# Second attention: transposes of the weights right ahead of the next scores, both token products of a cycle behind them in one piece

## The chip, the cores and the metric

One core of one Trainium2 chip runs the whole program. The time is that of one launch in device microseconds, the median of three runs. Five engines work side by side, each through its own list of instructions in order, and meet by semaphores alone: TensorE (PE, with its weight loads PEld), VectorE (DVE), ScalarE (ACT), GpSimd (POOL) and SyncE (SP, which issues DMAs).

## The reference, cut to what matters

Two transformer blocks over x of shape (2, 1024, 256), 16 heads of 16. Each has two attentions and an MLP. The change touches the second attention of the first block, and the products that run beside it:

```python
def _topk_cross_attn(h, ctx, w_q, b_q, w_kv, b_kv, w_co, b_co):
    ...                                    # q from 1024 tokens, k and v from 154 context rows
    scores = jnp.einsum('bqhd,bkhd->bhqk', q, k) / jnp.sqrt(jnp.float32(D)).astype(h.dtype)
    top_s, top_i = jax.lax.top_k(scores, TOPK)          # 16 largest of 154
    attn = jax.nn.softmax(top_s, axis=-1)
    vg = jnp.take_along_axis(v_bh[:, :, None, :, :], top_i[..., None], axis=3)
    o = jnp.einsum('bhqk,bhqkd->bqhd', attn, vg).reshape(B, L, C)
    return o @ w_co + b_co
```

## The kernel before, in words

All matrices are float32. The work of the four attentions and of the stages between them (output projection, layer norm, projections, MLP; "token work" below) is written as small steps. `make_plan` gives every step a due time with `plan.at` or `plan.fill`; `Plan.finish` sorts all steps by due time, ties by the order in which they were added, gives each PE step a PSUM bank, and every engine then walks the one sorted list and carries out its own part of each step. So the due times are no delays: they set nothing but the order in each engine's queue.

The second attention (`topk_run`) takes 64 cycles, one for each group of four heads and tile of 128 queries. Call them k = 0 to 63, and let k.5 be a due time half a cycle after the cycle's start (`step`, 5.2 in plan units). Of cycle k:

- PE, `c_scores` (L1156), due 0.8 cycle ahead: eight matmuls into two of the four banks 1 to 4, one bank for each half of the heads (hf 0 and 1). It waits until both banks have been left by the cycle two earlier: for VectorE's first replacement (L1575) and for `c_exp_all` of that cycle's second half.
- DVE, `c_top` at k.0 and k.5: largest eight, replace, largest eight, replace (L1572 to L1582) for two heads each. It waits for `c_neg` two halves back.
- ACT, `c_neg` (L1343) at k.12 and k.62, and `c_exp_all` (L1353) at k.25 and k.75: the negated maximum, and exp of all scores.
- POOL, `c_pick` (L1658, L1660) at k.55 and (k+1).05: keeps the weights of the picked scores.
- PE, `c_tail` and `c_turn` (L1167, L1175): transposes of the weights, into bank 7 and bank 5. ACT, `c_copy` (L1363, L1364), takes them out.
- After every fourth cycle PE `c_pv` (L1188, L1190) multiplies with the values into bank 7, ACT `o_copy` (L1338) takes the result out, PE `o_turn` (L986) transposes it, DVE `o_norm` (L1481, L1491) normalizes. The next `c_tail`, which writes bank 7 too, waits for `o_copy`.

The token work is put into these cycles by the helper `under` of `make_plan`: one slot a cycle in cycles 1 to 17 (`per` = 1), two a cycle in 19 to 63 (`per` = 2; call them A and B). A slot of the MLP is one product of four matmuls, `ua`, `ub` (both L1049) or `down` (L1064). What follows the product on ACT or DVE is in the same slot, but `fill` sets it later: by a quarter of a cycle for the kinds in `SOON` (ACT's copies: `ua_copy` L1298, `silu` L1314, `qk_a`, `v_copy`, `on_copy`, `modulate` L1264), by 0.9 for those in `LATE` (DVE's: `hid` L1527, `x_sum`, `stats`, `out_sum`, `qk_d` L1459), by half a cycle for `x_hat` (L1306). Token products use banks 0 and 6 here, as `o_turn` does. Where both still hold something whose follow-up stands later in the list, `finish` pulls that follow-up forward.

In cycles 19 to 35 and 36 to 52 the token work is the output projection and MLP of the first batch element (halves n = 0 and 1), from slot 0 at 19A and 36A: `on_turn` 0, `y_mm` 2 and 3, `x_hat` 5, `hat_turn` 7, `ua` 9 to 16 (with `silu` after the fourth and the eighth), `ub` 17 to 24, `down` 25 to 32. Three products of the next stage (`qk`) lie in slots 5, 6 and 8 of the second. Cycles 53 to 58 hold the rest of that stage, 59 to 63 the first ten slots for the second batch element.

Of the kernel before, what the change touches and what calls it, by code (L numbers as in the profile page):

```python
# [467 lines left out]
def topk_run(plan, start, step):  # L468


    u = 0
    for b in range(B):
        for half in range(2):
            for g in range(GB):
                gi = 8 + b * GB + g
                for t in range(4 * half, 4 * half + 4):
                    t0 = start + u * step
                    sooner = (9.0, 4.0)[u] if u < 2 else 0.0
                    plan.at(t0 - 0.8 * step - sooner, ("c_score", gi, t, 0), ("c_score", gi, t, 1), ("c_scores", gi, t))
                    for hf in range(2):  # L480
                        t1 = t0 + 0.5 * hf * step
                        plan.at(t1 - (sooner if u == 0 else 0.0), ("c_top", gi, t, hf))
                        plan.at(t1 + 0.12 * step, ("c_neg", gi, t, hf))
                        plan.at(t1 + 0.25 * step, ("c_exp_all", gi, t, hf))
                        plan.at(t1 + 0.55 * step, ("c_pick", gi, t, hf))
                    plan.at(t0 + 1.9 * step, ("c_tail", gi, t), ("c_turn", gi, t))
                    plan.at(t0 + 2.0 * step, ("c_copy", gi, t))
                    if t % 4 == 3:
                        plan.at(t0 + 2.3 * step, ("c_pv", gi, half))
                        plan.at(t0 + 2.75 * step, ("o_copy", gi, half))  # L490
                        plan.at(t0 + 3.1 * step, ("o_turn", gi, half))
                        plan.at(t0 + 3.6 * step, ("o_norm", gi, half))
                    u += 1
    return start + u * step


def first_slots():

    s, b = 1, 0
    qk = lambda n, u: ("qk", s, b, n, u)  # L500
    out = lambda n, u: ("qk_d" if u % 2 else "qk_a", s, b, n, u)
    turns = lambda n: [("hat_turn", s, b, n, k) for k in range(CK)]
    modulate = lambda n: [("modulate", s, b, n, k) for k in range(CK)]
    x_hat = lambda n: [("x_hat", s, b, 2 * n), ("x_hat", s, b, 2 * n + 1)]
    first = [[("stats", s, b, 0), ("stats", s, b, 1), ("rstd", s, b, 0)] + x_hat(0) + [("stats", s, b, 2), ("stats", s, b, 3), ("rstd", s, b, 1)],
             [("prep",), ("mcol", 0), ("mcol_add", 0)], turns(0), modulate(0) + x_hat(1), [qk(0, 0)], turns(1), [out(0, 0)], [qk(0, 2)],
             modulate(1), [out(0, 2), qk(1, 0)], [out(1, 0), qk(1, 2)], [out(1, 2)]]
    left = []
    for n in range(2):
        left += [[qk(n, 1)], [out(n, 1), qk(n, 3)], [out(n, 3)]]  # L510
        for t in range(4 * n, 4 * n + 4):
            left += [[("v", s, b, t)], [("v_copy", s, b, t)]]
    return first, left


def make_plan():
    plan = Plan()
    first, left = first_slots()
# [25 lines left out]
    step = 5.2  # L544
    A2 = end + 3
    half = 16 * step
    end = topk_run(plan, A2, step)
    plan.at(A2 - 1.9, ("load_row", 1), ("load_gate", 2), ("load_out", 2), ("gate_out", 2))
    plan.at(A2 + 4, ("load_gate", 3))

    def under(first, last, slots, per, aside=0.3):
        return plan.fill(slots, [A2 + (first + (i + aside) / per) * step for i in range(int((last - first) * per))], (0.25 * step, 0.9 * step, 0.5 * step))

    under(1, 18, joined([gap_slots(2, 1, n) for n in range(2)]), 1)
    under(1, 7, late, 1, 0.8)
    plan.at(A2 + 8.5 * step, ("stash",), ("load_w", "m1"), ("load_w", "m2a"))
    for part in range(4):
        plan.at(A2 + (9.3 + part) * step, ("gate_m2", 0, part))
    plan.at(A2 + 18 * step, ("load_row", 2), ("load_gate", 4), ("load_out", 3), ("gate_out", 3), ("load_gate", 5), ("load_row", 3))
    plan.at(A2 + 19 * step, ("load_w", "wb1"))  # L560
    under(19, 36, in_turn([gap_slots(3, 0, 0, 1)]), 2)
    mlp = in_turn([gap_slots(3, 0, 1, 1)])
    (head0, tail0), (head1, tail1) = gap_slots(4, 0, 0), gap_slots(4, 0, 1)
# [19 lines left out]
    first, second = ([(head, tail[0:4:2]) for head, tail in four], [tail[1:4:2] + tail[4:] for _, tail in four])  # L583
    blocks = joined([([], (head + tail)[10:]), three[1]] + first)
    where = plan.fill(blocks, early)
    last = [i for i, slot in enumerate(blocks) if ("ub", 3, 1, 1, HT - 1) in slot][0]
# [1289 lines left out]
```

## Time and profile before

| | us |
|---|---|
| median of 3 runs | 1485.85 (1484.37 to 1489.32) |
| the profiled execution's own time | 1483.23 |
| its span | 1481.4 |
| PE busy | 1366.8 (92%) |
| DVE busy | 902.6 (61%) |
| ACT busy | 725.3 (49%) |
| POOL busy | 345.4 (23%) |
| clock granted to TensorE, mean | 0.966 |

The second attention lies about between 190 and 573 us of the span. A busy share is that of all instructions of the engine, and says nothing of what waits for what; "idle before, releaser" in a row says how long the engine stood still ahead of an instruction, and whose instruction let it go.

### The profile page before, as it was taken

How to read it: one execution, taken by the hardware profiler on the slowest of the kernel's cores; microseconds unless marked ns; L12 is line 12 of the kernel's file. 1: busy time of each engine (PE TensorE's matmuls, PEld its weight loads, DVE VectorE, ACT ScalarE, POOL GpSimd, SP SyncE). 2: the span in 40 equal slices, each digit the busy share in tenths (PEclk: the TensorE clock that was granted, in tenths of full speed). 3: DMA queues.
4: the chain of work that ended last, by engine and by line, in shares of the span. 5: the costliest groups of instructions: out<-in, count | busy, mean ns of one | idle time of the engine just before them, and what ended most of it. 6: DMA issues, size and time to landing. Idle time of an engine off the chain costs nothing.

```text
span 1481.4 us, 25463 instructions
## 1 busy us (share of the span) xinstructions
PE 1366.8 (92%) x9100; PEld 685.4 (46%) x9100; DVE 902.6 (61%) x2787; ACT 725.3 (49%) x1482; POOL 345.4 (23%) x397
## 2 busy tenths in 40 slices
PE   7999987888998997989899999999999999988998
PEld 5467654444644553442224333343433335544665
DVE  3556488877777785865465666676676345650320
ACT  2354555574474363125544565554556664443221
POOL 1021078875665675010000100001010011010220
PEclk9999987899999899999999999999999999999999
DMA  5101003000000000000002000000000000000000
GB/s 194 47 26 27 21 19 115 10 1 1 4 13 1 30 2 27 0 2 0 2 0 73 1 1 1 2 1 2 1 12 1 2 2 2 13 6 0 15 24 23
DMA packets 22094, 26.75 MB, mean 18 GB/s; under 512 B 4205, under 2 KB 19635, under 8 KB 21709
## 3 DMA queue, kind: packets, MB, share of 16 engines
q1 hardware_dynamic: 21059, 25.03, 5.2%
q8 instruction: 73, 1.20, 0.4%
q14 instruction: 53, 0.43, 0.1%
q10 hardware_dynamic: 909, 0.10, 0.0%
HBM read 21.58 MB, written 3.08 MB: 17 GB/s over the span
## 4 chain that ended last, share of the span: by engine, by line
PE 78%; DVE 11%; ACT 4%; issue 4%; POOL 2%; DMA 0%; ACTq 0%; SPq 0%; DVEq 0%; POOLq 0%
PE bank L1092 27%; PE bank L1049 11%; PE bank L1132 8%; PE bank L1064 7%; PE bank L1028 6%; PE bank L1007 3%; PE bank L986 2%; PE bank L1156 2%; PE bank L1034 2%; PE bank L1175 2%; DVE left L1575 1%; DVE x_hat L1520 1%; DVE stats L1507 1%; PE bank L1014 1%; DVE left L1582 1%
## 5 line engine op out<-in xcount | busy, mean ns | idle before, releaser
L1331 ACT ACTIVATE pr<-bank 128x512 f32<-128x512 f32 x656 | 353.4, 598 | 282.3 <-PE bank L1092 269.0
L1547 DVE TENSOR_REDUCE part_max<-bank 128x1 f32<-128x512 f32 x512 | 327.2, 685 | 182.4 <-PE bank L1092 181.9
L1092 PE MATMUL bank<-slot 32*128 32x512 f32 (+1 forms) x3072 | 386.1, 519 | 10.5 <-ACT pr L1331 6.1
L1092 PEld LDWEIGHTS bank<-slot 32*128 32x128 f32 x3072 | 160.7, 185 | 209.1 <-issue 157.3
L1599 POOL TENSOR_SCALAR var_eps<-mean_var 128x4 f32<-128x4 f32 x24 | 5.5, 227 | 889.9 <-DVE mean_var L1511 889.4
L1658 POOL TENSOR_SCALAR left<-left 128x308 f32<-128x308 f32 x128 | 125.2, 978 | 83.9 <-ACT exp_all L1353 41.7
L1132 PE MATMUL bank<-pr,v 128*17 128x512 f32 x1024 | 135.2, 600 | 0.2
L1049 PE MATMUL bank<-h_t,w_m 128*128 128x512 f32 x256 | 128.7, 629 | 4.7 <-DVE o_all L1491 3.2
L1660 POOL TENSOR_TENSOR probs<-left,exp_all 128x308 f32<-128x308 f32 x128 | 107.2, 838 | 10.7
L1572 DVE MAX8 top<-bank 128x8 f32<-128x154 f32 x256 | 69.7, 314 | 48.4 <-PE bank L1156 36.9
L1353 ACT ACTIVATE exp_all<-bank,neg 128x154 f32<-128x154 f32 x256 | 85.6, 386 | 6.7 <-DVE left L1575 2.1
L1551 DVE TENSOR_REDUCE neg_max<-bank 128x3 f32<-128x462 f32 (+1 forms) x96 | 50.7, 579 | 52.1 <-PE bank L1092 51.8
L1575 DVE MATCH_REPLACE8 left<-top,bank 128x154 f32<-128x154 f32 x256 | 77.0, 309 | 0.0
L1582 DVE MATCH_REPLACE8 left<-top,left 128x154 f32<-128x154 f32 x256 | 76.0, 305 | 0.4 <-issue 0.3
L1049 PEld LDWEIGHTS bank<-h_t,w_m 128*128 128x128 f32 x256 | 45.6, 197 | 65.4 <-issue 58.0
L1500 DVE TENSOR_TENSOR x_sb<-x_sb,bank 128x512 f32<-128x512 f32 x32 | 21.9, 685 | 84.1 <-PE bank L1007 84.1
L1064 PE MATMUL bank<-w_m,hidden 128*128 128x256 f32 x256 | 66.7, 407 | 6.6 <-DVE hidden L1527 6.5
L1364 ACT ACTIVATE probs_t<-bank 128x512 f32<-128x512 f32 x64 | 38.2, 597 | 63.9 <-PE bank L1175 63.6
L1338 ACT ACTIVATE o_st<-bank 128x512 f32<-128x512 f32 x64 | 38.3, 599 | 61.2 <-PE bank L1137 30.1
L1578 DVE MAX8 top<-left 128x8 f32<-128x154 f32 x256 | 68.2, 309 | 0.0
L1007 PE MATMUL bank<-w_out,o_norm_t 128*128 128x256 f32 x256 | 64.4, 396 | 1.4 <-DVE x_sb L1500 1.4
L1028 PE MATMUL bank<-h_t,wa 128*128 128x512 f32 x128 | 63.6, 626 | 2.0 <-ACT h_t L1264 1.9
(143 smaller groups left out, 1767.0 us busy)
## 6 DMA issues: line engine op xcount, KB each, us to landing
w_m<-in_L_xcond_w_m SPq DMA_DIRECT2D x1, 2048.0 KB, 7.6
w_m<-in_L_xcond_w_m SPq DMA_DIRECT2D x2, 1024.0 KB, 7.8
w<-in_L_xcond_w SPq DMA_DIRECT2D x2, 1024.0 KB, 6.6
w_ada<-in_L_xcond_w_ada SPq DMA_DIRECT2D x1, 1792.0 KB, 9.9
x_sb<-in_x SPq DMA_DIRECT2D x6, 256.0 KB, 6.3
res_row<-rows_dram SPq DMA_DIRECT2D x12, 128.0 KB, 3.3
out_x<-x_sb SPq DMA_DIRECT2D x6, 256.0 KB, 2.1
wa<-in_L_xcond_w_qkv SPq DMA_DIRECT2D x1, 768.0 KB, 6.6
```

The lines of the kernel that those rows point to most:

```text
L1007: last = nc.tensor.matmul(bank[:, tt * C:(tt + 1) * C], m.o_norm_t[:, slot, k, tt * P:(tt + 1) * P], m.w_out[:, j % 2, k, :], start=(k == ...
L1028: last = nc.tensor.matmul(bank[:, :], w[:, k, c0:c0 + P], m.h_t[:, slot, k, :], start=(k == 0), stop=(k == CK - 1))
L1049: last = nc.tensor.matmul(bank[:, :], w[:, k, c0:c0 + P], m.h_t[:, slot, k, :], start=(k == 0), stop=(k == CK - 1))
L1064: last = nc.tensor.matmul(bank[:, tt * C:(tt + 1) * C], m.hidden[:, j, t * P:(t + 1) * P], w, start=(j == 0), stop=(j == HT - 1))
L1092: last = nc.tensor.matmul(g.bank(*tile)[:, into], left, right, start=True, stop=True)
L1132: last = nc.tensor.matmul(out[h * HW:h * HW + VE, :], m.v[b][:, d % TB, heads[h], :], m.pr[:, slots[h], :], start=(d % TB == 0), stop=(d % ...
L1331: nc.scalar.activation(m.pr[:, u % NPR, :], g.bank("s", gi, i)[:, :], ACT.Exp).then_inc(g.free("s", gi, i), 1)
L1547: nc.vector.tensor_reduce(m.part_max[:, slot, h * TB + i // 8, i // 4 % 2:i // 4 % 2 + 1], bank[:, :], axis=AX.X, op=ALU.max).then_inc(don ...
L1575: nc.vector.match_replace(m.left1[:, v % 2, hh, :], m.top[:, v % 2, hh, 0:8], bank[:, hh * C:hh * C + S2], -FAR).then_inc(m.left1_done, 1)
L1582: nc.vector.match_replace(m.left2[:, v % 4, hh, :], m.top[:, v % 2, hh, 8:16], m.left1[:, v % 2, hh, :], -FAR).then_inc(m.left2_done, 1)
L1658: nc.gpsimd.tensor_scalar(left, left, -FAR, None, ALU.is_equal).then_inc(m.marked, 1)
L1660: nc.gpsimd.tensor_tensor(m.probs[:, u % 2, 2 * hf:2 * hf + 2, 0:S2], left, m.exp_all[:, v % 4, :, :], ALU.mult).then_inc(m.pick_done, 1)
```

## The change

In `topk_run` the transposes of cycle k's weights move from (k+1).9 to (k+2).12, and their copy from (k+2).0 to (k+2).16. The product with the values moves from .3 to .42 of its cycle, its copy from .75 to .8, and `o_turn` from .1 to .14. In `under` slots A and B, which were due at .15 and .65 of a cycle, are due at .30 and .32; with one slot a cycle the due time stays .3. The instructions are the same.

```diff
-                    plan.at(t0 + 1.9 * step, ("c_tail", gi, t), ("c_turn", gi, t))
-                    plan.at(t0 + 2.0 * step, ("c_copy", gi, t))
+                    plan.at(t0 + 2.12 * step, ("c_tail", gi, t), ("c_turn", gi, t))
+                    plan.at(t0 + 2.16 * step, ("c_copy", gi, t))
                     if t % 4 == 3:
-                        plan.at(t0 + 2.3 * step, ("c_pv", gi, half))
-                        plan.at(t0 + 2.75 * step, ("o_copy", gi, half))
-                        plan.at(t0 + 3.1 * step, ("o_turn", gi, half))
+                        plan.at(t0 + 2.42 * step, ("c_pv", gi, half))
+                        plan.at(t0 + 2.8 * step, ("o_copy", gi, half))
+                        plan.at(t0 + 3.14 * step, ("o_turn", gi, half))
                         plan.at(t0 + 3.6 * step, ("o_norm", gi, half))
...
     def under(first, last, slots, per, aside=0.3):
-        return plan.fill(slots, [A2 + (first + (i + aside) / per) * step for i in range(int((last - first) * per))], (0.25 * step, 0.9 * step, 0.5 * step))
+        return plan.fill(slots, [A2 + (first + i // per + aside + 0.02 * (i % per)) * step for i in range(int((last - first) * per))], (0.25 * step, 0.9 * step, 0.5 * step))
```

## Rows read from the trace of the kernel before

**Rows 1.** Stretches of the second attention: start:end, length, busy us of each engine, clock

```profile
215.00:285.00 70.00, 54.34 (x389) 30.39 (x389) 62.25 (x349) 42.76 (x121) 59.94 (x67) 0.88 0.20 66
285.00:410.00 125.00, 113.48 (x654) 65.98 (x652) 99.00 (x515) 69.35 (x179) 82.78 (x94) 0.89 0.01 2
```

**Rows 2.** Waits between 215 and 590 us: us in total, times, longest

```profile
POOL left L1658 <- ACT exp_all L1353: 41.7, 19, 7.6
DVE top L1572 <- PE bank L1156: 36.9, 22, 6.2
...
PE bank L1014 <- ACT x_hat L1306: 6.6, 3, 3.3
```

**Rows 3.** TensorE's timeline, one cycle of the MLP: start, us, instructions

```profile
443.65 0.42 PE L1167 MATMUL bank<-ident,probs 128*32 128x128 f32 x8
...
444.50 1.88 PE L1049 MATMUL bank<-h_t,w_m 128*128 128x512 f32 x4
446.31 0.79 PE L1156 MATMUL bank<-kc,slot 32*128 32x154 f32 x8
447.03 1.98 PE L1049 MATMUL bank<-h_t,w_m 128*128 128x512 f32 x4
448.95 0.42 PE L1167 MATMUL bank<-ident,probs 128*32 128x128 f32 x8
```

**Rows 4.** VectorE's timeline: two halves of `c_top` after one another

```profile
254.36 0.54 DVE L1572 MAX8 top<-bank 128x8 f32<-128x154 f32 x2
...
256.41 0.55 DVE L1572 MAX8 top<-bank 128x8 f32<-128x154 f32 x2
```

**Rows 5.** TensorE's timeline: transposes before scores, and two token products in one piece

```profile
244.58 0.66 PE L1175 MATMUL bank<-ident,probs 128*128 128x128 f32 x4
245.16 0.79 PE L1156 MATMUL bank<-kc,slot 32*128 32x154 f32 x8
...
590.32 3.70 PE L1049 MATMUL bank<-h_t,w_m 128*128 128x512 f32 x8
```

**Rows 6.** ScalarE's timeline in cycle 27 and 28, with two silus

```profile
335.72 0.69 ACT L1298 ACTIVATE hidden<-bank,columns 128x512 f32<-128x512 f32 x1 [0.33 <-PE bank L1049]
...
337.72 2.00 ACT L1314 ACTIVATE hidden<-hidden 128x1024 f32<-128x1024 f32 x2
339.63 0.19 ACT L1343 ACTIVATE neg<-top 128x2 f32<-128x2 f32 x1
339.83 1.28 ACT L1353 ACT_TABLE_LOAD   x1
341.13 0.67 ACT L1353 ACTIVATE exp_all<-bank,neg 128x154 f32<-128x154 f32 x2
```

**Rows 7.** TensorE's timeline in the same cycles; [idle before <-releaser]

```profile
335.61 0.79 PE L1156 MATMUL bank<-kc,slot 32*128 32x154 f32 x8
...
341.94 0.79 PE L1156 MATMUL bank<-kc,slot 32*128 32x154 f32 x8 [0.96 <-ACT exp_all L1353]
```

**Rows 8.** TensorE after a product with the values, no token product behind it

```profile
300.54 0.43 PE L1167 MATMUL bank<-ident,probs 128*32 128x128 f32 x8 [0.81 <-ACT o_st L1338]
```

**Rows 9.** TensorE at two token products that stand still

```profile
365.05 1.19 PE L1064 MATMUL bank<-w_m,hidden 128*128 128x256 f32 x2 [3.08 <-DVE hidden L1527]
...
511.47 3.78 PE L1034 MATMUL bank<-wa,h_t 128*128 128x256 f32 x8 [2.82 <-DVE slot L1459]
```

**Rows 10.** ScalarE and VectorE at waits in cycles 9 and 13

```profile
238.58 0.69 ACT L1276 ACTIVATE slot<-bank,columns 128x512 f32<-128x512 f32 x1 [3.32 <-PE bank L1028]
...
264.21 0.55 DVE L1572 MAX8 top<-bank 128x8 f32<-128x154 f32 x2 [3.45 <-ACT neg L1343]
```

**Rows 11.** TensorE in cycle 13

```profile
258.52 2.08 PE L1188 MATMUL bank<-tails_t,vt 128*128 128x512 f32 x2
...
261.87 1.09 PE L1014 MATMUL bank<-ident,x_hat 128*128 128x128 f32 x8
```

**Rows 12.** The stretch behind the stall at 365 us, as in Rows 1

```profile
365.00:371.00 6.00, 5.95 (x23) 4.35 (x24) 1.85 (x12) 0.52 (x2) 0.00 (x0) 0.54 0.01 3
```

## Prediction

> **What bounds the kernel now.** I read first the busy shares by stretch [rows 1]. In the cycles with one token slot VectorE is the busiest (62.25 of 70 us), in those with two TensorE is (113.48 of 125). The sums of waits [rows 2] show that the engines also wait in a ring: VectorE 36.9 us for scores, GpSimd 41.7 us for ScalarE's exp. Where a wait costs time must then be read from the queue orders and timelines.
>
> A cycle of the MLP without a stall [rows 3] is 448.95 − 443.65 = 5.30 us of TensorE, back to back: transposes 0.85 (0.35 + 0.50), token product 1.81, scores 0.72, token product 1.92. VectorE has 2 × 2.05 = 4.1 us of `c_top` in a cycle [rows 4] and needs more than that only with `ub`, where `hid` comes on top. So in `ua`, `qk` and `down` slots TensorE is the bound, and any new gap in it is lost.
>
> **The change part by part.** No instruction is added or removed, no DMA, and nothing moves on SP's queue. On POOL only `rstd` and `row` move, with their slots.
>
> *TensorE's work.* By the due times, two-slot cycles go from [transposes, A, scores, B] to [transposes, scores, A, B]. Transposes to scores take 0.35 + 0.58, two products in one piece 3.63 (3.70 less the 0.07 by which a row overlaps the next) [rows 5], scores 0.72: 5.28 against 5.30. The new piece is worth −0.02 a cycle, 0 to −1 over 45 cycles. In one-slot cycles TensorE's order stays, but for the values product (below).
>
> *The exp behind the token copies.* Scores of cycle k+2 need `c_exp_all` of (k, second half), due k.75. Before, slot A's ACT copy was due k.40 and B's k.90, behind that exp. Now they are due k.55 and k.57, both ahead of `c_neg` (k.62) and the exp. B's copy can only start when B is done, and TensorE has nothing but the transposes (0.93) left before it wants the scores. A copy starts 0.11 after its product (335.72 − 335.61) and takes 0.69, of which 0.09 overlaps what follows (339.72 − 339.63); `c_neg` takes 0.20, exp 0.67, and scores follow its end by 0.14 (341.94 − 341.80) [rows 6, 7]. That is 1.72 against 0.93: about 0.78 us of new stall in every cycle whose last token product has an ACT copy behind it. Such are 23, 24, 26, 40, 43, 63 (`ua`): 6 × 0.78 = 4.7. Nine more have a modulate, `qk_a`, `v_copy` or `on_copy` last (22, 36, 38, 39, 54, 55, 58, 59, 62), 0.8 to 1.5 each: 8.3. Sum 13. The ends are 0, if TensorE waits there for something later anyway, and 20.
>
> *The same with silu.* In cycles 25, 27, 42, 44 slot A has two silus with a table load, and the exp behind them needs a load back. From the copy's start to the scores let go, 341.94 − 335.72 = 6.22 [rows 6, 7]. Before, TensorE filled this with scores, B, transposes and the next A, and stood still 0.96 (1.07 at the most in the four). Now scores come before A and the next A is behind the next scores, so only B and the transposes (1.82 + 0.93) cover it: 0.11 + 6.22 − 2.75 = 3.6 us. Where B is a `ua`, its copy adds 0.6 (cycle 42: 4.2). In cycle 25 the values product covers some, but the next `c_tail` then waits for `o_copy` behind the exp: 3.5. Extra over before: 2 × 2.6 + 3.1 + 2.4 = 10.7. Ends 6 and 13.
>
> The trace has 1.28 us for the load, and the exp starts 0.02 after it [rows 6]. The Trainium skill (ScalarE: Activation LUTs, What ACT_TABLE_LOAD costs) has about 2.66 us for a switch, drain included. By that the four stalls would be some 2 × 1.38 longer each, 11 more; the row decides, and I take nothing for it.
>
> *Values product behind the tokens.* It was due .3, ahead of B; now .42, behind both, and the next `c_tail` in bank 7 wants its `o_copy` at once. Without a token product behind it this costs 0.81 [rows 8]. In cycles 29, 33, 37, 41, 45, 49, 53, 57 B covered it: 8 × 0.8 = 6.5. Ends 3 (VectorE-bound `ub` cycles swallow it) and 6.5.
>
> *Gains, one-slot cycles.* At .3 the values product and the token product tied, the former first; now the token product goes first. In cycle 13 the `hat_turn` leaves at 258.5 instead of 261.87, which frees `c_neg` and takes 3.3 of VectorE's 3.45; in 9 `qk` leaves the values product (2.0 at full clock) sooner and shortens ACT's wait of 3.32 by as much [rows 10, 11]. Gain 5.3. `c_copy` also moves behind the first `c_neg`; I count nothing for that. Ends 2 and 8.
>
> *Gains, scores ahead of a product that stands still.* At 365.05 `down` waits 3.08 for the last `hid` [rows 9], which is behind the `c_top` of those scores. Now scores no longer wait for A: up to 1.9 back, in both halves: 3.8. At 511.47 the `v` products stand 2.82 with scores behind them, and these go ahead now; together with cycle 36 I take 3.5. Sum 7.3, ends 2 and 10.
>
> *Gains, layer norm.* Both `stats` now come ahead of `c_top`'s second half, so `x_hat` is ready about one half (2.05) sooner; TensorE waits 6.6 for it in three places [rows 2], of which two are long: 4. Ends 0 and 5. What is late next there is the exp behind the modulates, counted above.
>
> *Clock.* Behind the 3.08 stall the granted clock is 0.54, near the lower level of 1.2 GHz, and 5.95 us of matmuls there cost some 3 us more than at 2.4 GHz [rows 9, 12]. Four new stalls of about 3.5 come, three of 2.5 to 3 shrink: +2, ends −8 and +12. The Trainium skill (TensorE: Matmul & The Clock Gate, HAM oscillation) says too that idle gaps of the array put it back to half rate; by it alone each of the four would be followed by a slow stretch, +12, as the fourth case below.
>
> Sum: 13 + 10.7 + 6.5 − 5.3 − 7.3 − 4 + 2 = +15.6. The profiled execution took 1483.23 (span 1481.4 and 1.8 around it), so 1498.8; it lies 2.6 under the median of the runs shown, so the median forecast is 1485.85 + 15.6 = 1501.5.
>
> **The rivals.**
>
> 1. *Faster: the scores are what the ring waits for.* VectorE waits 36.9 us for them in 22 waits [rows 2], and scores now leave one token product (1.8) sooner after the transposes. If each wait loses that and the exps are in time, 22 × 1.8, halved since TensorE is the bound in half of them, gives −20, and with the +5 of the values product −15: 1471. For it: the long waits. Against: in the gapless cycle TensorE has no idle time to give, and the exp's new place is plain in the due times. It decides if `c_exp_all` (k, second half) ends before the transposes do.
> 2. *No change.* The columns are the same and the new stalls fall where VectorE is late anyhow: costs at their low ends (0 + 6 + 3), gains 9: ±4 about 1486.
> 3. *Slower, by half.* ScalarE's stalls are there, but gains are at their upper ends (8 + 10 + 5) against 30: +7, 1493.
> 4. *Slower, with the clock.* All four silu stalls and some others drop the clock for a stretch like that of rows 12, and the gains are at their low ends: 30 + 12 − 10 = +32, 1518.
>
> **How the numbers follow.** Chances: forecast 0.42, rival 1 0.11, rival 2 0.12, rival 3 0.2, rival 4 0.15. A run can be told from no change at about 0.3% (4.5 us), so slower takes the forecast, 3 and 4 with a little of 2: 0.79; same 0.1; faster 0.11. The range leaves out rival 1 and the far end of 4: 1484 to 1518.
>
> **What would show it.** In the profile after: scores (L1156) let go by ACT `exp_all` with total idle of over 15 us instead of 5, four of them 3 to 4 us long right behind the silus; `c_tail` let go by `o_st` about 0.8 us each time; no wait of VectorE for `c_neg` at cycle 13; two products of 3.63 in one piece. It is wrong if `exp_all` still ends before the transposes in `ua` cycles, or if the time is within 4 us of before with these stalls in place, which would mean that VectorE was the bound in those cycles.

## The result and the profile after

The changed kernel takes 1510.88 us (median, 1505.44 to 1514.02) against 1486.52 of the kernel before: ratio 1.0156, 95% interval [1.0128, 1.0184], 24 us slower. The forecast was 1501.5 (range 1484 to 1518), slower with a chance of 0.79. Sign and mechanism came as forecast. The size did not: 15.6 forecast, about 24 measured, with terms that were off both ways. Two of the errors offset each other: the values product was put 4.5 us too high, which hid that much of the 9.4 us by which the gains were too high. That much of the forecast's nearness is luck.

The changed kernel's waits in the second attention (190 to 600 us; us in total, times, longest), beside [rows 2]:

```profile
POOL left L1658 <- ACT exp_all L1353: 47.4, 17, 6.8
...
PE bank L1156 <- ACT exp_all L1353: 21.5, 16, 4.3
...
DVE top L1572 <- ACT neg L1343: 16.4, 9, 4.3
...
PE bank L1167 <- ACT o_st L1338: 13.5, 13, 3.8
DVE top L1572 <- PE bank L1156: 12.2, 8, 3.4
```

and those of the same lines that [rows 2] leaves out for the kernel before:

```profile
DVE top L1572 <- ACT neg L1343: 10.8, 8, 3.4
...
PE bank L1156 <- ACT exp_all L1353: 5.9, 8, 1.1
PE bank L1167 <- ACT o_st L1338: 4.2, 4, 1.8
```

VectorE's wait for scores fell from 36.9 to 12.2 us. A reader who takes this line for the bound would have called the change a success. It is not: the wait has moved to TensorE, ahead of the scores (5.9 to 21.5) and of the transposes (4.2 to 13.5).

Cycle 27 after, ScalarE and then TensorE, answers to [rows 6, 7]:

```profile
341.76 0.69 ACT L1298 ACTIVATE hidden<-bank,columns 128x512 f32<-128x512 f32 x1 [1.86 <-PE bank L1049]
342.46 1.28 ACT L1314 ACT_TABLE_LOAD   x1
343.76 2.00 ACT L1314 ACTIVATE hidden<-hidden 128x1024 f32<-128x1024 f32 x2
345.67 0.19 ACT L1343 ACTIVATE neg<-top 128x2 f32<-128x2 f32 x1
345.87 1.28 ACT L1353 ACT_TABLE_LOAD   x1
347.17 0.67 ACT L1353 ACTIVATE exp_all<-bank,neg 128x154 f32<-128x154 f32 x2
```

```profile
343.72 0.66 PE L1175 MATMUL bank<-ident,probs 128*128 128x128 f32 x4
347.98 0.97 PE L1156 MATMUL bank<-kc,slot 32*128 32x154 f32 x8 [3.60 <-ACT exp_all L1353]
```

From the copy's start to the scores it is 347.98 − 341.76 = 6.22 us, as before; less of TensorE's work lies beside it, so the gap is 3.60 instead of 0.96. The other three with silus are 3.60 and 4.28 ahead of scores, and in cycle 25 3.76 ahead of the transposes.

A plain cycle with an ACT copy last, TensorE and then ScalarE:

```profile
337.52 0.66 PE L1175 MATMUL bank<-ident,probs 128*128 128x128 f32 x4
339.01 0.79 PE L1156 MATMUL bank<-kc,slot 32*128 32x154 f32 x8 [0.83 <-DVE left L1575]
```

```profile
337.28 0.69 ACT L1298 ACTIVATE hidden<-bank,columns 128x512 f32<-128x512 f32 x1 [1.03 <-PE bank L1049]
337.86 0.19 ACT L1343 ACTIVATE neg<-top 128x2 f32<-128x2 f32 x1
338.09 0.67 ACT L1353 ACTIVATE exp_all<-bank,neg 128x154 f32<-128x154 f32 x2
```

The gap is 0.83 (0.78 forecast). Its releaser is named as VectorE's replacement, the other semaphore that the scores wait for. But the exp ends at 338.76 and the scores start 0.25 later, behind copy, neg and exp. So the 21.5 us of the waits are not all that belongs to the exp, and part of what is put down to VectorE is the exp's.

### The profile page after: what moved, and what is told of

Read it like the earlier page. It is cut to its first block, busy times and chain, and to the rows that moved or that the text cites. A ratio compares the mean times of both kernels' runs of the same rounds, so it can differ in the third digit from the quotient of the medians.

```text
span 1503.6 us, 25463 instructions
## 1 busy us (share of the span) xinstructions
PE 1362.9 (91%) x9100; PEld 685.0 (46%) x9100; DVE 901.8 (60%) x2787; ACT 723.1 (48%) x1482; POOL 345.9 (23%) x397
## 3 DMA queue, kind: packets, MB, share of 16 engines
HBM read 21.58 MB, written 3.08 MB: 16 GB/s over the span
## 4 chain that ended last, share of the span: by engine, by line
PE 72%; DVE 12%; issue 5%; ACT 4%; POOL 4%; DMA 2%; SPq 0%; ACTq 0%; POOLq 0%; DVEq 0%
PE bank L1092 26%; PE bank L1049 10%; PE bank L1132 8%; PE bank L1064 6%; PE bank L1028 5%; PE bank L1007 3%; PE bank L986 2%; DVE left L1575 2%; DVE left L1582 2%; DVE top L1572 1%; PE bank L1156 1%; POOL left L1658 1%; PE bank L1034 1%; DVE x_hat L1520 1%; PE bank L1014 1%
## 5 line engine op out<-in xcount | busy, mean ns | idle before, releaser
L1092 PE MATMUL bank<-slot 32*128 32x512 f32 (+1 forms) x3072 | 388.1, 522 | 10.5 <-ACT pr L1331 6.1
L1660 POOL TENSOR_TENSOR probs<-left,exp_all 128x308 f32<-128x308 f32 x128 | 107.5, 840 | 10.7
L1572 DVE MAX8 top<-bank 128x8 f32<-128x154 f32 x256 | 69.5, 314 | 28.8 <-ACT neg L1343 16.4
L1156 PE MATMUL bank<-kc,slot 32*128 32x154 f32 x512 | 54.5, 332 | 25.1 <-ACT exp_all L1353 21.5
L1630 POOL TENSOR_TENSOR x_sb<-x_sb,res_row 128x512 f32<-128x512 f32 x48 | 60.2, 1276 | 22.4 <-DMA res_row<-rows_dram 15.6
## 6 DMA issues: line engine op xcount, KB each, us to landing
w_ada<-in_L_xcond_w_ada SPq DMA_DIRECT2D x1, 1792.0 KB, 10.8
```

The lines of the kernel that those rows point to most:

```text
L1092: last = nc.tensor.matmul(g.bank(*tile)[:, into], left, right, start=True, stop=True)
L1660: nc.gpsimd.tensor_tensor(m.probs[:, u % 2, 2 * hf:2 * hf + 2, 0:S2], left, m.exp_all[:, v % 4, :, :], ALU.mult).then_inc(m.pick_done, 1)
```

## The experiments

Times are medians; where a difference is small, it is read from ratios to the kernel before, whose median in these series was 1484.8 to 1486.3. A stretch or a wait is read from the one profiled execution of each kernel.

**exp_first.** The changed kernel, with the second half's neg and exp ahead of the token copies.

```diff
-                        plan.at(t1 + 0.12 * step, ("c_neg", gi, t, hf))
-                        plan.at(t1 + 0.25 * step, ("c_exp_all", gi, t, hf))
+                        plan.at(t1 + (0.12, 0.03)[hf] * step, ("c_neg", gi, t, hf))
+                        plan.at(t1 + (0.25, 0.04)[hf] * step, ("c_exp_all", gi, t, hf))
```

> The changed kernel with one more edit: c_neg and c_exp_all of a cycle's second half due at k.53 and k.54, ahead of both token copies (k.55, k.57). TensorE's, VectorE's and GpSimd's orders stay as in the changed kernel. Theory (the exp behind the token copies and silus holds up the scores): TensorE's idle time ahead of the scores until ACT exp_all falls from 21.5 us to under 4, the four gaps of 3.6 to 4.3 us go, and the time falls by 16 to 24 us, to about 1491; the 0.8 us gaps for o_st stay. Rival A (VectorE's placement of the hids and sums, both behind the first half of c_top, is what costs): 1505 or more. Rival B (the place of the transposes or TensorE's new order costs by itself): 1505 or more.

1481.08 us, ratio 0.9965 [0.9951, 0.9978]: 30 us under the changed kernel, more than the 16 to 24 expected, and 0.35% faster than the kernel before. TensorE's, VectorE's and GpSimd's orders are the changed kernel's, so neither the transposes' place nor the hids' is the cost (rivals A and B). The edit also puts the exp ahead of the copies in the one-slot cycles, where the change had moved nothing; before_exp_first below has that part too, and gains nothing. TensorE in cycles 27 and 28:

```profile
334.49 0.79 PE L1156 MATMUL bank<-kc,slot 32*128 32x154 f32 x8
335.22 3.70 PE L1049 MATMUL bank<-h_t,w_m 128*128 128x512 f32 x8
338.85 0.42 PE L1167 MATMUL bank<-ident,probs 128*32 128x128 f32 x8
339.20 0.66 PE L1175 MATMUL bank<-ident,probs 128*128 128x128 f32 x4
339.79 0.79 PE L1156 MATMUL bank<-kc,slot 32*128 32x154 f32 x8
```

No gap: 339.79 − 334.49 = 5.30. On ScalarE the exp at 335.88 is now done before the copy and its silus begin:

```profile
335.88 0.67 ACT L1353 ACTIVATE exp_all<-bank,neg 128x154 f32<-128x154 f32 x2
337.24 0.69 ACT L1298 ACTIVATE hidden<-bank,columns 128x512 f32<-128x512 f32 x1 [0.69 <-PE bank L1049]
```

**silu_late.** The changed kernel, only the silus moved behind that exp.

```diff
-                self.at(time + (later[2] if step[0] == "x_hat" ...
+                self.at(time + (later[3] if step[0] == "silu" and len(later) > 3 else later[2] if step[0] == "x_hat" ...
...
-... (0.25 * step, 0.9 * step, 0.5 * step))
+... (0.25 * step, 0.9 * step, 0.5 * step, 0.6 * step))
```

> The changed kernel with the silus of the second attention's token slots due 0.6 of a cycle behind their slot (k.90) instead of 0.25 (k.55), so behind neg and exp of the second half; the token copies stay ahead of them. TensorE's and VectorE's orders stay. Theory: of the four long gaps (3.6, 3.6, 4.3, 3.8 us, of which 0.7 to 0.8 is the copies' own) about 12 us go, and some clock with them: 1511 - 12 to 16, about 1497; exp_all still holds the scores for about 10 us in the other cycles. Rival D (all of the 30 us that exp first gave back came from the silus): about 1482. Rival E (the copies alone): 1508 or more.

1493.31 us, ratio 1.0036 [1.0022, 1.0049]. So the silus' share is 1.0156 − 1.0036 = 1.20%, 17.8 us, and the copies' the other 0.71%, 10.5 us (to exp_first). Both are clear of their intervals, rivals D and E fall. TensorE's wait for `exp_all` is now in gaps of 2.35 at the most:

```profile
PE bank L1156 <- ACT exp_all L1353: 12.5, 15, 2.3
```

TensorE's list is the same in both kernels, so the same stretches can be laid side by side. From one values product to the next around the silus of cycles 25 and 27, the changed kernel and then silu_late:

```profile
323.68 1.05 PE L1190 MATMUL bank<-probs_t,vc 128*17 128x512 f32 x8
360.14 1.05 PE L1190 MATMUL bank<-probs_t,vc 128*17 128x512 f32 x8
```

```profile
328.61 1.05 PE L1190 MATMUL bank<-probs_t,vc 128*17 128x512 f32 x8
354.66 1.05 PE L1190 MATMUL bank<-probs_t,vc 128*17 128x512 f32 x8
```

That is 36.46 against 26.05 us. Around those of cycles 42 and 44, between the transposes behind two values products, it is 37.39 against 29.35. Together the silus cost 18.4 us here, close to the 17.8 of the ratios. 11.2 of it are gaps (17.6 against 6.4), and the other 7.2 are slower matmuls behind them: two token products in one piece took 4.93 to 5.63 us instead of 3.70.

**tokens_only and transposes_only.** Each half of the change alone on the kernel before: the edit of `under`, and the edit of `topk_run`, as in the diff above.

> The kernel before with the edit of under alone: both token slots due at .30 and .32, transposes, copies and values product where they were before. The values product (tied at .3, added first) then goes ahead of both token products, so that these cover its copy. Theory: exp behind the token copies as in the changed kernel, so most of the loss is there: 1486.5 + 17 = about 1503 (24.4 measured, less 13.5 us of waits for o_st that go, plus what cycles 9 and 13 gained). TensorE idles over 15 us ahead of the scores until exp_all, and under 6 ahead of the transposes until o_st. Rival B (the transposes' new place costs): within 4 us of 1486.5.

> The kernel before with the edit of topk_run alone: transposes, their copy, values product, its copy and o_turn at the new due times, token slots at .15 and .65 as before. Token slot B then stands behind the values product and covers its copy, and the exp of the second half stands behind slot A's copy only. Theory: no loss, 1480 to 1489, some of it faster by cycles 9 and 13. Rival B (the transposes' place costs): 1495 or more.

tokens_only takes 1514.58 (ratio 1.0191 [1.0170, 1.0211]), transposes_only 1480.70 (0.9954 [0.9937, 0.9971]). All the loss is in the token slots' due times; the edit of `topk_run` is by itself a gain of 0.46%. The product of both ratios is 1.0144, the changed kernel's is 1.0156 ± 0.0028.

The plan's lists tell what each half does. With the tokens at .15 and .65 the move of the transposes to .12 passes nothing in TensorE's list until the last cycle. It is the new place of slot A that gives [transposes, scores, A, B]. What transposes_only changes for TensorE is the place of the values product in cycles 9 and 13, and the end of the attention: one `ua` goes ahead of the last transposes, one ahead of the last `o_turn`. For ScalarE it changes the places of `c_copy` and `o_copy`. This order at the end had no term in the prediction. In the kernel before TensorE has a wait there, for `o_norm`:

```profile
587.34 1.98 PE L1049 MATMUL bank<-h_t,w_m 128*128 128x512 f32 x4 [3.18 <-DVE o_all L1491]
```

It stands, 3.18 long, in all five kernels without the edit of `topk_run`, and in none of the nine with it. From the first scores of cycle 63 to the end of the span the five take 924.5 to 928.0 us, the nine 917.5 to 921.7. No run has the end's order alone.

tokens_only was expected at 1503, and 1514.58 is well above it: it has the same wait for the exp as the changed kernel, and more of VectorE's for neg (16.4 there). How much of the 11 us each makes is not shown:

```profile
DVE top L1572 <- ACT neg L1343: 29.8, 14, 4.9
PE bank L1156 <- ACT exp_all L1353: 22.0, 17, 4.3
...
PE bank L1167 <- ACT o_st L1338: 9.5, 7, 3.6
```

I had also expected its wait for `o_st` under 6, it is 9.5; a 3.6 us piece is left, since the copy (`o_copy`) is itself behind the silus in cycle 25.

**values_between and exp_first_values_between.** The values product between the two token products, in the changed kernel and in exp_first.

```diff
-                        plan.at(t0 + 2.42 * step, ("c_pv", gi, half))
+                        plan.at(t0 + 2.31 * step, ("c_pv", gi, half))
```

> The changed kernel with the values product at 2.31, between the two token products of its cycle (in one-slot cycles still behind the token product); all else as changed. The prediction's term: the second token product covers o_copy again, -6.5 (-3 at the least), about 1505. Rival H (the copy of the product still stands behind the late exp in ScalarE's queue, and what is gained ahead of the transposes is lost ahead of the scores): within 3 us of the changed kernel.

> exp_first with the values product at 2.31, so that it stands between the two token products of its cycle. Theory: against exp_first the 0.8 us gaps ahead of the transposes until o_st go in eight cycles, -5 to -8 us, to about 1484, near the kernel before or a little under it. Rival C (those gaps are swallowed, since VectorE or ScalarE is as late): within 2 us of exp_first.

1506.01 (ratio 1.0142 [1.0115, 1.0170]) against the changed kernel's 1.0156, and 1478.94 (0.9953 [0.9938, 0.9969]) against exp_first's 0.9965. Both gains are about 2 us, and neither is clear of its interval; the second still leaves no room for the 6.5 us (0.44%) of the term. The gaps are there and 0.81 long, as in [rows 8], with two token products ahead (changed kernel):

```profile
360.14 1.05 PE L1190 MATMUL bank<-probs_t,vc 128*17 128x512 f32 x8
362.00 0.42 PE L1167 MATMUL bank<-ident,probs 128*32 128x128 f32 x8 [0.81 <-ACT o_st L1338]
```

In exp_first they sum to 13.4 us, and moving the product takes 5.3 of these away, but the time moves by 2. Where the other 3 us went I did not trace.

**before_exp_first and transposes_exp_first.** The same two lines as in exp_first, on the kernel before and on transposes_only.

> The kernel before with c_neg and c_exp_all of the second half due at k.53 and k.54; only ScalarE's order changes, by passing slot A's copies and silus (k.40 of an .15 slot stays ahead; o_copy and c_copy of later cycles fall behind the exp). Theory: the copy of slot A is still ahead of the exp, so the 0.96 us stalls at the silus stay, and only o_copy (k.75) goes behind the exp: 1486 with -1 to -4. Rival F (exp early is worth most of 30 us in any order of TensorE): 1470 or less.

> The edit of topk_run alone (transposes_only) with the second half's neg and exp at k.53 and k.54. Slots A and B stay at .15 and .65. Theory: the exp was in time already, so it adds little to transposes_only: 1477 to 1482. Rival F (exp early is a gain of its own): 1472 or less.

1489.06 (1.0020 [1.0005, 1.0035]) and 1481.53 (0.9966 [0.9953, 0.9980], transposes_only has 0.9954). So an early exp is no gain of its own: rival F falls in both, and the 30 us of exp_first are the removal of what the change brought in. On the kernel before it even costs 0.2%, where I had expected a small gain; why is open. Within the second attention its profile is longer by 5.0 us in cycles 0 to 17 (102.8 against 97.8) and by 0.6 in the others, and tokens_only, with the lists of the kernel before in these cycles on every engine, took 102.7 there: a single profile says little about them.

**copies_only.** The kernel before with `c_copy` at 2.16 and `o_copy` at 2.8.

> The kernel before with only c_copy at 2.16 and o_copy at 2.8 of the cycle; every other engine's order is that of the kernel before. Theory (VectorE waited 10.8 us for c_neg, behind c_copy; what transposes_only gained is this): 1479 to 1484. Rival G (transposes_only gained from the token products of cycles 9 and 13 going ahead of the values product): within 2 us of 1486.

1488.51 (1.0021 [1.0008, 1.0034]): my theory of what transposes_only gained was wrong, and even its sign. VectorE's wait for neg hardly moved, 10.8 to 9.1 us, so the run doesn't say what that wait is worth.

**copy_ahead_of_neg.** The reverse, on exp_first_values_between: `c_copy` at 2.13 and the first half's `c_neg` at .14.

> exp_first_values_between with c_copy ahead of the first half's c_neg again, as it was before the change; only ScalarE's order changes. copies_only was 2 us slower than before with c_copy behind c_neg: if that holds here, -2, about 1477. If the transposes now come so late that c_neg waits for them and VectorE for c_neg, +2 or more.

1477.56 (0.9939 [0.9921, 0.9958]) against 0.9953: 2 us in the same direction, inside the intervals.

**before_token_first_9_13.** The kernel before, `c_pv` at 2.31 for the first 17 cycles alone.

```diff
-                        plan.at(t0 + 2.3 * step, ("c_pv", gi, half))
+                        plan.at(t0 + (2.31 if u < 17 else 2.3) * step, ("c_pv", gi, half))
```

> The kernel before with the token products of cycles 9 and 13 ahead of the values product; nothing else is moved on any engine. The prediction's term: -5.3, about 1481. Rival I (GpSimd is busy back to back from the arrival of the second MLP weights in cycle 9 to cycle 14, and sets the pace there): within 2 us of 1486.

1482.21 (0.9980 [0.9967, 0.9994]): a gain of 3 us, 1 to 5, of the 5.3 forecast. This and copies_only are two of the three parts of transposes_only: 0.9980 × 1.0021 = 1.0001, against 0.9954 for the whole. So what is left, 0.47% or 7 us, points at the third, the end of the attention, where the profiles differ by 4.0. GpSimd in the changed kernel in cycle 9:

```profile
239.59 1.27 POOL L1645 TENSOR_TENSOR w_m<-w_m,gate_row 128x512 f32<-128x512 f32 x1 [2.46 <-DMA w_m<-in_L_xcond_w_m]
240.95 0.98 POOL L1658 TENSOR_SCALAR left<-left 128x308 f32<-128x308 f32 x1
242.01 0.84 POOL L1660 TENSOR_TENSOR probs<-left,exp_all 128x308 f32<-128x308 f32 x1
242.93 0.98 POOL L1658 TENSOR_SCALAR left<-left 128x308 f32<-128x308 f32 x1
```

It works back to back once the DMA has landed, and the transposes of these cycles wait for it. So rival I holds in part: a sooner token product frees ScalarE and VectorE, but GpSimd limits what follows. Counted from the first `c_top`, that of cycle 11 starts 3.5 us sooner than in the kernel before, that of cycle 14 no sooner.

**transposes_silu_late.** transposes_only with the silus 0.63 of a cycle behind their slot, thus behind the exp in the order of before.

> transposes_only with the silus due 0.63 of a cycle behind their slot, so behind the second half's exp; TensorE's order stays. Theory: the four stalls of about 1 us that the silus cost in the order of before go: 1480.7 - 2 to 5, about 1477, the fastest so far. If the ub products then wait for the later silus, it is 1481 or more.

1471.30 us, ratio 0.9911 [0.9889, 0.9934]: 0.9% faster than the kernel before and the fastest of all. The stall of [rows 7] is gone; TensorE in the same cycles:

```profile
335.19 0.79 PE L1156 MATMUL bank<-kc,slot 32*128 32x154 f32 x8
335.91 1.98 PE L1049 MATMUL bank<-h_t,w_m 128*128 128x512 f32 x4
337.83 0.43 PE L1167 MATMUL bank<-ident,probs 128*32 128x128 f32 x8
338.19 0.65 PE L1175 MATMUL bank<-ident,probs 128*128 128x128 f32 x4
338.68 1.88 PE L1049 MATMUL bank<-h_t,w_m 128*128 128x512 f32 x4
340.49 0.79 PE L1156 MATMUL bank<-kc,slot 32*128 32x154 f32 x8
```

The gain over transposes_only is 0.43%, 6.4 us, and by the intervals 2 to 11; 2 to 5 were expected.

## Why the prediction was right or wrong

*TensorE's work.* Right: pieces of 3.70 in the rows, and 5.30 for a gapless cycle in either order.

*The exp behind the copies*, 13. Right in kind and near in size: 0.83 a cycle, 10.5 us in all by silu_late against exp_first.

*The same with silu*, 10.7. The gaps were right: 15.2 us after, 4.0 in the same places before, 11.2 extra. But the share by the chip is 17.8, and I had put the clock elsewhere, in a term of its own. Stretches behind three of the four gaps, columns as in [rows 1] (the third column from the end is the clock):

```profile
348.00:354.00 6.00, 6.00 (x19) 2.67 (x19) 3.00 (x14) 1.83 (x7) 5.42 (x6) 0.72 0.01 3
457.00:463.00 6.00, 6.00 (x18) 2.39 (x16) 2.14 (x12) 0.83 (x2) 2.47 (x3) 0.66 0.00 0
328.00:334.00 6.00, 5.50 (x26) 3.66 (x27) 2.88 (x15) 1.60 (x5) 3.63 (x4) 0.50 0.00 0
```

At a clock of 0.50 to 0.72 a stretch of 6 us holds 1.7 to 3 us of slowdown. The fourth, after 474 us, has 0.72 too. By this estimate the four cost about 8.5. In silu_late TensorE had the full clock at three of these places and 0.72 at the fourth, behind its gap of 2.35, which leaves about 7, as the two kernels side by side gave (7.2).

*Clock*, +2. Too small, and put at the wrong place: the clock alone makes 7 of the silus' 17.8. Over the whole run it is less. The mean granted clock is 0.969 in the profile after and 0.966 in the one before, but that is the fastest of the four runs; their mean is 0.9665, against 0.9687 in 26 runs of the kernel before (0.964 to 0.975). I estimate +4 us from it, (1 − clock) × span being 50.5 against 46.5, and this is not clear of the spread. The Trainium skill's rule that idle gaps put TensorE back to half rate (TensorE: Matmul & The Clock Gate, HAM oscillation) fits the four gaps: each had slow matmuls behind it. Taken as I had taken it, for idle gaps as such, it did not hold everywhere. Behind the 3.37 us gap at 500 us the clock is 1.00:

```profile
500.00:506.00 6.00, 5.73 (x38) 4.51 (x39) 4.14 (x25) 2.41 (x7) 0.98 (x1) 1.00 0.02 4
```

*Values product*, 6.5. Gap of 0.81 right, its worth not: about 2, and 5 at the most by the interval of exp_first_values_between.

*Gains, one-slot cycles*, 5.3. Measured 3 (1 to 5) in the order of before. In the changed kernel's profile the stretch from the first scores to those of cycle 18 took 96.6 us against 97.8. That is 1.2 less, where profiles of one order differ by 5.

*Gains, scores ahead of a product that stands still*, 7.3. Failed for the larger part. At `down` behind the eighth `ub`, VectorE and TensorE after:

```profile
368.53 1.40 DVE L1527 SCALAR_TENSOR_TENSOR hidden<-bank,columns,hidden 128x512 f32<-128x512 f32 x2
369.84 0.54 DVE L1572 MAX8 top<-bank 128x8 f32<-128x154 f32 x2
...
371.89 0.54 DVE L1572 MAX8 top<-bank 128x8 f32<-128x154 f32 x2
...
373.94 0.74 DVE L1527 SCALAR_TENSOR_TENSOR hidden<-bank,columns,hidden 128x512 f32<-128x512 f32 x1
```

```profile
369.40 1.98 PE L1049 MATMUL bank<-h_t,w_m 128*128 128x512 f32 x4
374.93 1.66 PE L1064 MATMUL bank<-w_m,hidden 128*128 128x256 f32 x5 [3.55 <-DVE hidden L1527]
```

The last `hid` is behind both halves of `c_top` in VectorE's list, which runs without a gap. So sooner scores don't bring it forward: 3.55 against 3.08 [rows 9]. I had argued that the scores started that chain, where VectorE was simply busy. The wait of the second `down`, at 500 us, also grew (3.37; 3.08 before). The `v` stall did shrink, 2.82 to 1.74:

```profile
536.12 1.17 PE L1034 MATMUL bank<-wa,h_t 128*128 128x256 f32 x2 [1.74 <-DVE slot L1459]
```

*Gains, layer norm*, 4. `hat_turn` waits 0.9 us for ACT's `x_hat`, once, where it was 6.6 us in three places before. Its waits for other releasers grew by 2.1 in sum (over the whole run), so 3.6 us of waiting are gone; what that is worth in time no run isolates.

The books, in us: for copies, silus and clock I had 13 + 10.7 + 2 = 25.7, and exp_first gives 28.4 (1.91%): +2.7. For the values product 6.5 against 2: −4.5. For the gains 16.6; exp_first, which has the gains and the values product but not the rest, is 5.2 under the kernel before, so the gains are 5.2 + 2 = 7.2: +9.4. Together +7.6, and 15.6 + 7.6 = 23.2 of the 24 measured. The gains here are what is left over, so the books would close with any split.

The profiles tell where that remainder comes from. Time from the first scores of one cycle to those of another:

| cycles | before | changed | exp_first |
|---|---|---|---|
| up to the scores of 0 | 179.2 | 180.8 | 181.2 |
| 0 to 18 | 97.8 | 96.6 | 97.3 |
| 18 to 36 | 113.7 | 122.1 | 111.3 |
| 36 to 53 | 109.7 | 123.8 | 111.7 |
| 53 to 63 | 56.5 | 58.7 | 55.0 |
| 63 to the end | 924.5 | 921.7 | 919.2 |

The loss is in the two MLP halves, 8.4 and 14.1 us. Of the 7.2 of gains, 3 to 5 fall behind the scores of cycle 63. I had forecast 2 there, one of the two long waits for `x_hat`, but not the wait for `o_norm`; in transposes_only, where that wait for `x_hat` stays, the stretch is 4.0 shorter all the same. In the cycles before, for which I had forecast 14.6, 2 to 4 came. The step that failed is the gains, and in it "scores ahead of a product that stands still"; the end of the attention was left out. Rival 4 had the low gains and the clock behind the silus right, but not its size.

## What to carry to other kernels

In a plan of due times, regrouping one engine's work also moves all follow-ups: compare each follow-up's new place with every wait in its own engine's list, above all ahead of a table load. Here a move of a third of a cycle at most put two copies ahead of an exp, and 30 us hung on that order alone. Look at the lists themselves, and at their ends too: the new place of the transposes passed nothing in TensorE's list for 63 cycles, and took a 3.18 us wait away in the last.

Ask of a long wait whether its engine is the one that is late. VectorE's wait for scores fell by two thirds while the kernel became slower, and behind the four long gaps of TensorE the lower clock cost again about half to four fifths of their length (1.7 us behind 3.60, 3 behind 3.76).

## What the runs showed of the hardware

The table load took 1.28 us and the exp began 0.02 later, in the rows of every kernel shown, with nothing between the two. And the length of a gap of TensorE did not settle the clock behind it: behind 3.60 us it was 0.72 over 6 us, behind 3.37 us 1.00, and behind 2.35 us, in silu_late, 0.72 again (454.58 to 460.63 us).
